# Inverse softmax divisors by broadcast loads from DRAM instead of products on TensorE

## The reference

```python
q, k, v = X @ Wq, X @ Wk, X @ Wv              # 16 heads of queries, 8 of keys and values, 64 wide
q, k = rope(q), rope(k)                       # each key head serves 2 query heads
att = 50 * tanh(q k^T / 16 / 50)              # causal
att = softmax(att)
x = layernorm(X + (att v) @ Wo)
q8 = per_token_int8(x)                        # scale = max|x| / 127
x = layernorm(x + float16((q8 @ weight^T) * in_scale * w_scale + bias))
```

## Time and profile before

| | us |
|---|---|
| median of 3 runs | 1320.56 (1318.67 to 1322.78) |
| the profiled execution | 1322.9, span 1321.2 |
| TensorE matmuls busy | 1272.4 (96% of the span), 5840 of them |
| weight loads busy | 936.2 (71%) |
| VectorE busy | 1038.7 (79%) |
| ScalarE busy | 901.4 (68%) |
| GpSimd busy | 377.7 (29%) |
| mean granted TensorE clock | 0.989 of 2.4 GHz |

### The profile page before, as it was taken

How to read it: one execution, slowest core, us unless ns; L and a number is a source line. 1 busy time by engine, 2 the same in 40 slices (tenths; PEclk the granted TensorE clock), 3 DMA queues, 4 the chain that set the end, 5 groups by cost and what they waited for, 6 DMA issues and landing times.

```text
span 1321.2 us, 17006 instructions
## 1 busy us (share of the span) xinstructions
PE 1272.4 (96%) x5840; PEld 936.2 (71%) x5840; DVE 1038.7 (79%) x1314; ACT 901.4 (68%) x1019; POOL 377.7 (29%) x438
## 2 busy tenths in 40 slices
PE   6899999999999999999999999999999999999896
PEld 5677777767766777677776777767777677777573
DVE  3588988983679888896478988898556988888566
ACT  4278787862677777875368867687447777879464
POOL 4232231111751111111383111111147211112165
PEclk9899999999999999999999999999999999999898
DMA  9683736495724464748551654466762355353551
GB/s 317 140 280 101 175 113 168 119 243 152 189 69 107 113 149 99 203 92 244 159 152 65 152 112 124 96 184 182 206 185 80 93 139 110 104 116 119 148 142 56
DMA packets 112401, 191.44 MB, mean 145 GB/s; under 512 B 19382, under 2 KB 65980, under 8 KB 104764
## 3 DMA queue, kind: packets, MB, share of 16 engines
q1 hardware_dynamic: 107564, 179.88, 52.1%
q10 hardware_dynamic: 4752, 10.49, 2.1%
HBM read 84.67 MB, written 38.54 MB: 93 GB/s over the span
## 4 chain that ended last, share of the span: by engine, by line
PE 83%; DVE 7%; issue 3%; ACT 3%; DMA 2%; POOL 1%; SPq 1%; POOLq 0%; DVEq 0%; ACTq 0%
PE ps L829 27%; PE ps L749 19%; PE ps L803 17%; PE ps L873 11%; PE ps L770 6%; PE ps L893 1%; PE ps L849 1%; DVE prob_lo L1292 1%; DVE prob_hi L1288 1%; DMA div<-y_scratch 1%; DVE xT L1208 1%; DVE stats L1370 1%; ACT probs L1032 1%; ACT probs L1027 0%; PE ps L883 0%
## 5 line engine op out<-in xcount | busy, mean ns | idle before, releaser
L829 PE MATMUL ps<-prob_hi,v 128*65 128x512 f32 (+3 forms) x1280 | 410.7, 371 | 8.4 <-DVE prob_lo L1292 8.4
L1027 ACT ACTIVATE probs<-ps 128x1024 f32<-128x1024 f32 x288 | 293.6, 1019 | 133.3 <-PE ps L803 133.3
L1292 DVE TENSOR_TENSOR prob_lo<-probs,prob_hi 128x1024 fp32r<-128x1024 f32 x288 | 360.0, 1250 | 9.8
L1535 POOL TENSOR_SCALAR_AFFINE_SELECT probs<-probs 128x256 f32<-128x256 f32 (+1 forms) x192 | 155.6, 818 | 705.3 <-ACT probs L1032 705.3
L803 PE MATMUL ps<-qk 128*128 128x512 f32 (+1 forms) x1280 | 314.5, 372 | 3.0 <-issue 1.8
L1032 ACT ACTIVATE probs<-probs 128x1024 f32<-128x1024 f32 x288 | 305.7, 1061 | 8.6
L749 PE MATMUL ps<-xT,w_ring 128*128 128x512 f32 x1152 | 286.9, 393 | 4.3 <-issue 4.3
L803 PEld LDWEIGHTS ps<-qk 128*128 128x128 f32 x1280 | 224.6, 189 | 62.6 <-issue 3.8
L1288 DVE CAST prob_hi<-probs 128x1024 fp32r<-128x1024 f32 x285 | 203.9, 715 | 79.7 <-POOL probs L1535 48.1
L749 PEld LDWEIGHTS ps<-xT,w_ring 128*128 128x128 f32 x1152 | 215.7, 189 | 50.9 <-issue 5.8
L829 PEld LDWEIGHTS ps<-prob_hi,v 128*65 128x65 f32 (+1 forms) x1280 | 170.7, 135 | 98.7 <-DVE prob_lo L1292 14.6
(11 more groups left out here) (92 smaller groups left out, 964.1 us busy)
## 6 DMA issues: line engine op xcount, KB each, us to landing
qk<-work_r SPq DMA_DIRECT2D x64, 512.0 KB, 8.8
qk<-work_r SPq DMA_DIRECT2D x256, 128.0 KB, 2.7
y_scratch<-sums SPq DMA_DIRECT2D x128, 130.0 KB
y_raw<-y_scratch SPq DMA_DIRECT2D x64, 256.0 KB, 4.3
wo<-wo_scratch SPq DMA_DIRECT2D x7, 2048.0 KB, 8.7
w_ring<-w_scratch SPq DMA_DIRECT2D x12, 1024.0 KB, 6.9
x_raw<-X_T SPq DMA_DIRECT2D x16, 512.0 KB, 6.7
x_in<-X SPq DMA_DIRECT2D x32, 256.0 KB, 4.3
```

What stands on the lines that cost most here:

```text
L829: mm = nc.tensor.matmul(sums_ps[:, :, GQ - w:GQ], v[:, kt, v0:v0 + width], p[:, at, col:col + REP * w].rearrange("p (h q) -> p h q", h=REP ...
L1027: nc.scalar.activation(probs[:, prob_place(g), :], scores[:, g % 2, :], ACT.Tanh, scale=SCORE_SCALE / SOFTCAP).then_inc(capped, 1)
L1292: nc.vector.tensor_tensor(prob_lo[:, prob_place(g), :], probs[:, prob_place(g), :], prob_hi[:, hi_place(g), :].bitcast(F32), ALU.subtract) ...
L1535: nc.gpsimd.affine_select(out=diag, in_=diag, compare_op=ALU.is_ge, fill=0.0, base=0, pattern=[[0, n], [1, P]], channel_multiplier=-1).the ...
```

## The change

`load_rows` now loads each head's row of inverse divisors, in fp32, to all 64 partitions of that head (a DRAM access pattern with step 0 over the partitions), so two DMAs of 256 KB per tile instead of two of 8 KB. There is one buffer `rows` of 128 x 8 x 128 fp32 for all tiles, so `load_rows(t)` waits for `scale_y(t - 1)`. `scale_y` multiplies `y_raw` by `rows` in SBUF. `invert` is the reciprocal alone, and `store_inverse` stores `div` in one DMA. `spread`, its set-up on GpSimd, VectorE and SP, and `spread_rows` are gone. On SP `load_rows(b, 1)` moves behind `put_sums` and `load_div` (in the last batch behind `put_sums(G - 2)`), and in the loop `load_rows(t + 3)` takes the place of `load_rows(t + 4)`. Two waits are renamed: `score(b, 1)` waits for `capped` of the batch before instead of its last `scale_y`, and the `rescale` of the last two tiles waits for the last `scale_y` instead of the last spread.

```diff
-    r_scratch = nc.dram_tensor("r_scratch", [2, G, KO * REP * GQ], F32, kind="Internal").ap()
+    r_scratch = nc.dram_tensor("r_scratch", [G, KO * REP * GQ], F32, kind="Internal").ap()
...
-        rows = over("rows", "work", [P, KO * P], F32R)
+        rows = over("rows", "work", [P, KO, P], F32)
...
             def store_inverse(b, c):
-                sp.wait_ge(inverse_lo, divs_upto(b, c))
-                for part in range(2):
-                    sp.dma_start(r_scratch[part, c].rearrange("(p n) -> p n", p=P),
-                                 inverse[:, part, :].bitcast(F32)).then_inc(div_stored[c], 16)
+                sp.wait_ge(inverse_done, divs_upto(b, c))
+                sp.dma_start(r_scratch[c].rearrange("(p n) -> p n", p=P), div[:, c, :]).then_inc(div_stored[c], 16)
...
             def load_rows(b, t):
-                sp.wait_ge(div_stored[t // 2], 32 * (b + 1))
-                if t >= 2:
-                    sp.wait_ge(rows_spread, rows_upto(b, t - 2))
-                for part in range(2):
-                    r0 = rows_at(t) + REP * part
-                    sp.dma_start(rows[r0:r0 + REP, :].rearrange("h (k n) -> h k n", k=KO).bitcast(F32),
-                                 r_scratch[part, t // 2].rearrange("(k h t n) -> t h k n", k=KO, h=REP, t=2)[t % 2]
-                                 ).then_inc(rows_loaded[t % 2], 16)
+                sp.wait_ge(div_stored[t // 2], 16 * (b + 1))
+                if t >= 1:
+                    sp.wait_ge(y_scaled, rows_upto(b, t - 1))
+                for h in range(REP):
+                    row = r_scratch[t // 2].rearrange("(k h t n) -> h t k n", k=KO, h=REP, t=2)[h, t % 2]
+                    sp.dma_start(rows[h * HD:(h + 1) * HD, :, :],
+                                 row.unsqueeze(0).broadcast_to([HD, KO, P])).then_inc(rows_loaded, 16)
...
                     load_rows(b, 0)
-                load_rows(b, 1)
                 store_inverse(b, 1)
...
                     load_div(b, 3)
+                    load_rows(b, 1)
                     load_y(b, 2)
                     for t in range(XRING):
                         load_x(b, t)
                     load_rows(b, 2)
-                    load_rows(b, 3)
                 else:
+                    load_rows(b, 1)
                     load_y(b, 2)
-                    load_rows(b, 2)
                     load_div(b, 2)
                     load_x(b, 0)
                     put_sums(b, NKV - 1, G - 1)
-                    load_rows(b, 3)
+                    load_rows(b, 2)
                     load_div(b, 3)
                     load_x(b, 1)
...
-                    if t + 4 < NT:
-                        load_rows(b, t + 4)
+                    if t + YRING < NT:
+                        load_rows(b, t + YRING)
...
-            def spread_rows(b, t):
...
-                for e in range(2):
-                    mm = nc.tensor.matmul(ps[:, spread_bank(b, t) + e, :], spread[rows_at(t):rows_at(t) + 2 * REP, :],
-                                          rows[rows_at(t):rows_at(t) + 2 * REP, e * 512:(e + 1) * 512], start=True, stop=True)
-                mm.then_inc(rows_spread, 1)
...
             def invert(b, c):
                 dve.wait_ge(div_loaded[c], 16 * (b + 1))
                 nc.vector.reciprocal(div[:, c, :], div[:, c, :]).then_inc(inverse_done, 1)
-                dve.wait_ge(inverse_done, divs_upto(b, c))
-                if divs_upto(b, c) > 1:
-                    before = divs_upto(b, c) - 2
-                    dve.wait_ge(div_stored[before % G], 32 * (before // G + 1))
-                nc.vector.tensor_copy(inverse[:, 0, :], div[:, c, :]).then_inc(inverse_hi, 1)
-                dve.wait_ge(inverse_hi, divs_upto(b, c))
-                nc.vector.tensor_tensor(inverse[:, 1, :], div[:, c, :], inverse[:, 0, :].bitcast(F32),
-                                        ALU.subtract).then_inc(inverse_lo, 1)
 
             def scale_y(b, t):
-                dve.wait_ge(rows_spread, rows_upto(b, t))
+                dve.wait_ge(rows_loaded, 32 * rows_upto(b, t))
                 dve.wait_ge(y_loaded[t % YRING], 2 * ring_upto(b, t, YRING))
                 row = y_raw[:, y_place(t), :, :].rearrange("p k n -> p (k n)")
-                nc.vector.tensor_tensor(row, ps[:, spread_bank(b, t):spread_bank(b, t) + 2, :].rearrange("p a c -> p (a c)"), row,
+                nc.vector.tensor_tensor(row, rows[:, :, :].rearrange("p k n -> p (k n)"), row,
                                         ALU.mult).then_inc(y_scaled, 1)
```

More of the change, by code:

```diff
@@ L168, in attention_block @@
         ident = over("ident", "div", [P, P], F32)
-        inverse = sb("inverse", [P, 2, P // G], F32R)
-        spread = sb("spread", [P, P], F32R)
-        spread_f32 = over("spread_f32", "prob_hi", [P, P], F32)
         ident16 = sb("ident16", [P, P], BF16)
@@ L191, in attention_block @@
         ps = ctx.enter_context(nc.psum_tensor("ps", [P, 8, 512], F32))
-        SPREAD_BANK, PV_BANK, PROJ_BANK = 2, 4, 6
+        PV_BANK, PROJ_BANK = 4, 6
         scores = ps[:, 0:4, :].rearrange("p (a h) c -> p a (h c)", a=2)
@@ L259, in attention_block @@
         inverse_done = sem("inverse_done")
[L260 to L266, removed]
+        rows_loaded = sem("rows_loaded")
         y_loaded = [sem(f"y_loaded{n}") for n in range(YRING)]
@@ L370, in v_bank @@
             return (PROJ_BANK + t % 2) if b == 0 or t < 2 or t >= NT - 2 else t % 2
[L373 to L378, removed]
         def row_tile(t):
@@ L591, in _ @@
             sp.dma_start(ffn_raw[:, :, :], ffn_weight_T.rearrange("(k p) c -> p k c", p=P)).then_inc(ffn_raw_in, 16)
-            sp.wait_ge(spread_set, 1)
-            for r0 in (REP, 32, 32 + REP):
-                sp.dma_start(spread[r0:r0 + REP, :].bitcast(F32), spread[0:REP, :].bitcast(F32)).then_inc(spread_ready, 16)
             sp.wait_ge(wv_hi_done, 2)
@@ L796, in score @@
                 elif g == 1:
-                    pe.wait_ge(y_scaled, rows_upto(b - 1, NT - 1))
+                    pe.wait_ge(capped, scores_upto(b - 1, NB - 1))
                 else:
@@ L928, in _ @@
                 weigh(b, NB - 2)
-                if not more:
-                    spread_rows(b, 0)
                 weigh(b, NB - 1)
@@ L936, in _ @@
                     project_v(b + 1, 3)
-                    spread_rows(b, 0)
                     project_v(b + 1, 4)
                     project_v(b + 1, 5)
-                spread_rows(b, 1)
                 if more:
@@ L945, in _ @@
                 for t in range(NT):
-                    if 1 <= t < NT - 1:
-                        spread_rows(b, t + 1)
                     for third in range(3):
@@ L1358, in rescale @@
                 if t >= NT - 2:
-                    dve.wait_ge(rows_spread, rows_upto(b, NT - 1))
+                    dve.wait_ge(y_scaled, rows_upto(b, NT - 1))
                 elif t >= FRING:
@@ L1389, in norm2 @@
                                         ).then_inc(normed, 1)
-            dve.wait_ge(spread_made, 2)
-            nc.vector.tensor_copy(spread[0:REP, :], spread_f32[0:REP, :]).then_inc(spread_set, 1)
             dve.wait_ge(const_made, 3)
@@ L1569, in _ @@
             nc.gpsimd.memset(one[:, :], 1.0).then_inc(const_made, 1)
-            nc.gpsimd.memset(spread_f32[0:REP, :], 1.0).then_inc(const_zero, 1)
-            pool.wait_ge(const_zero, 5)
+            pool.wait_ge(const_zero, 4)
             for i in (ident, ident16):
@@ L1574, in _ @@
                                         pattern=[[-1, P]], channel_multiplier=1).then_inc(const_made, 1)
-            nc.gpsimd.affine_select(out=spread_f32[0:REP, :], in_=spread_f32[0:REP, :], compare_op=ALU.is_ge, fill=0.0,
-                                    base=0, pattern=[[1, P]], channel_multiplier=-HD).then_inc(spread_made, 1)
-            pool.wait_ge(spread_made, 1)
-            nc.gpsimd.affine_select(out=spread_f32[0:REP, :], in_=spread_f32[0:REP, :], compare_op=ALU.is_ge, fill=0.0,
-                                    base=HD - 1, pattern=[[-1, P]], channel_multiplier=HD).then_inc(spread_made, 1)
             split_wk(0)
```

## The result

| | before | after |
|---|---|---|
| median of 3 runs, us | 1320.56 | 1369.48 (1365.73 to 1375.52) |
| ratio to before | | 1.0368, 95% interval 1.0326 to 1.0410 |
| profiled execution, us | 1322.9, span 1321.2 | 1365.7, span 1364.0 |
| TensorE busy | 1272.4 | 1258.1 |
| mean granted clock | 0.989 | 0.977 |

Slower by 3.7%. Lines of the kernel after: `load_rows` L492, `scale_y` L1260, `round_y` L1013, `round_v` L952, `split_v` L1165, `invert` L1254, `load_div` L478, `put_sums` L557, `project_out` L831, `turn_q` L841, `rescale` L1306, `residual2` L1501 and L1503, `w_scale` L689.

What follows compares the result with a forecast made beforehand. TensorE, busy 96% of the span, was taken to bound the kernel. Three batches at +9.3 us (+27.9) and the last at +0.6 gave +28.5 us, so 1320.6 + 28.5 = 1349 us; range 1325 to 1388.

Steps and rivals of the forecast that it cites:

- Products, 0.7 us a pair, 22 us at most: TensorE's 64 spread matmuls: each of 32 removed pairs gains 0.7 us where TensorE waits for nothing, 22 us at most.
- Start-up: 0: Kernel start: the removed set-up work on spread lies under the first loads, so it gains 0.
- Lock of the two SBUF inputs: Tile loop: scale_y with two SBUF inputs and GpSimd's add block each other; +0.4 us per batch for four tiles.
- tends to 7.65: Tiles with a residual2 and a scale_y: period no less than about 7.1 us, tending to 7.65, against 7.41.
- -0.6: Two tiles behind the weights' stretch in batches 0 to 2: pairs 6 and 7 against the lock, -0.6 us per batch.
- Row load 4.9 us from the first issue: Each tile's pair of row loads, priced like y_raw's loads: 4.9 us from the first issue to landing.
- Seam +3.1 in each batch: Batches 0 to 2: split_v(6) behind scale_y(1), which waits for rows(1), makes project_out(0) 3.1 us later.
- Clock, "a coin's toss, so +1.0": Seam: TensorE's idle 4.6 us may halve its clock, costing about 2 us; counted as +1.0 per batch.
- pair 2, -0.7: Batches 0 to 2, behind the seam's wait: removing pair 2 of the spread products gains 0.7 us.
- Weights +6.5 per batch with the clock: Batches 0 to 2: rows(4) and rows(5) collide with 2 MB of weights, +5.6 us, plus +0.9 for another idle stretch.
- Last batch +0.6: Last batch, without seam or weights: +2.1 for bytes, -0.5 shorter inversion, -1.4 pairs 2 and 3, +0.4 lock.
- slow reading of one place: Rival, chance 0.25: reading one DRAM place is slow; 1374 us at 150 GB/s, about 1415 at 104 GB/s.

Runs made afterwards that it cites:

- e1: Changed kernel without row loads, y multiplied by two PSUM banks (result not divided by the sums): 0.9824 of the kernel before, 1299.1 us.
- e2: Changed kernel without row loads, y multiplied by the cosine table in SBUF (result not divided by the sums): 0.9936 of the kernel before, 1312.7 us.
- e3: Changed kernel with all row loads and waits, but y multiplied by two PSUM banks instead of the rows: 1.0334 of the kernel before, 1365.6 us.
- e6: Changed kernel with all four weight loads asked for ahead of load_rows(4): 1.0378 of the kernel before, 1372.3 us.
- e9: Changed kernel, split_v/round_v(6, 7) ahead of scale_y(1)/round_y(1), w_scale and bias ahead of load_rows(4), wk and wq at t = 4: 1.0092, 1333.1 us.
- e8: Changed kernel, row loads reading 64 different rows of y_scratch, y multiplied by the cosine table: 1.0323 of the kernel before, 1364.7 us.
- e7: Changed kernel, each row load cut to one of eight pieces (64 KB per tile), y multiplied by the cosine table: 1.0150, 1343.5 us.
- e10: Changed kernel with rows(1), (4) and (5) of batches 0 to 2 issued by ScalarE on its own queue: 1.0285 of the kernel before, 1357.7 us.
- e11: Changed kernel, rows(1) ahead of div(2), e9's weight order; last batch div(1) ahead of rows(0), second buffer for odd rows: 1.0043, 1327.1 us.

## Why the prediction was right and wrong

Right in sign and in the main in mechanism (order, meeting, clock); 1349 us was 20 us too low, and 1369.5 lies within 1325 to 1388. Point by point:

- *Products, 0.7 us a pair, 22 us at most*: right of the tile, 0.8 us where nothing else holds it up. e1's 23 us are in part luck: 9 of them lie at the start and ahead of the last tile loop.
- *Start-up: 0*: this was 2 us too little a gain. The first of the 288 `prob_lo` starts at 61.3 instead of 63.1, the last of batch 0 2.0 us sooner; of the change, only the set-up of `spread` lies there, though no run takes it out alone:

```profile
L1244 DVE TENSOR_TENSOR prob_lo<-probs,prob_hi x288: 1218/1226/2202, 61.3 to 1276.4; 128x1024 fp32r<-128x1024 f32 x144
```

- *Lock of the two SBUF inputs*: "tends to 7.65" was measured at 7.67 and 7.68 us, and e2 and e3 show it on and off. The sum took it at +0.4 us per batch for four tiles; from turn_q(3) to turn_q(6) the loop lost 0.5 to 0.9 us where the sum had -0.6 for the part of it. That is 3.7 us too little over three batches. 1.3 of them are the size: I counted 7.51 per tile, between the ends of 7.1 and 7.65, and it was the upper end. The other 2.4 are a slip in the sum: by 7.51 against 7.41 two such tiles cost +0.2 us, and -0.6 stands there.
- *Row load 4.9 us from the first issue*: 5.55 in batch 0's seam (315.37 to 320.92); it was issued 0.56 us sooner than forecast, so `project_out(0)` started at 324.59, with 324.7 forecast. TensorE idled 6.7 us instead of 4.6 because it was done 2.2 us sooner than I had it, nearly all of it the start-up's 2.0.
- *Seam +3.1 in each batch*: this step failed, and batch 0's +3.0 is luck. From the last `prob_lo` of a batch to `project_out(0)` the seam is 5.0, 4.6 and 6.2 us longer than before; in batch 0 the start-up's 2.0 us hide that, in batches 1 and 2 the scores add 0.6 each. I set the new order against batch 0's times of before and left out that the 512 KB of rows(0) now stand ahead of `wo` and `put_sums`, on which div(2) waits. Batch 1, SP's queue, before and after:

```profile
625.17 0.41 SPq L577 DMA_DIRECT2D y_scratch<-sums  x1
...
632.80 0.32 SPq L495 DMA_DIRECT2D div<-y_scratch  x1
```

```profile
638.29 0.40 SPq L557 DMA_DIRECT2D y_scratch<-sums  x1
...
647.58 0.32 SPq L478 DMA_DIRECT2D div<-y_scratch  x1
```

  7.6 us have become 9.3 (7.4 and 8.4 in batch 0, 7.6 and 9.7 in batch 2), and rows(1) is behind that. Against the loops before, 14.9 us in place of 9.3: 5.6 us too little.
- *Clock, "a coin's toss, so +1.0"*, and *pair 2, -0.7*: the clock fell in every one of the three seams and cost 2.35, 2.3 and 1.5 us. Pair 2 gave nothing there: from `project_out(0)` to turn_q(0) the kernel before and e1 both take 12.34 us. Together 5.3 us too little, 3.2 of the clock and 2.1 of the pair. The half price had no row behind it; the trace of before had one idle stretch of that length and a fall behind it.
- *Weights +6.5 per batch with the clock*: 7.1, 3.6 and 6.7 us; 2.1 us too much in all. The size was right, the path only in part: I had only y(5) and rows(5) in it, and left out that `rescale(0)` waits for `w_scale` ahead of `scale_y(4)` (4.9, 3.2, 3.2 us). e6 and e9 show that this is a wait of its own.
- *Last batch +0.6*: 2.4 us; 1.8 too little. Up to `project_out(0)` it is +1.4 (div(1) took 11.5 us to its use instead of 10.1), about the forecast's 2.1 - 0.5. The step left out is the one behind it, +1.3 up to turn_q(0): div(3) stands behind rows(1) and rows(2) on SP's queue, rows(2) waits for `scale_y(1)` (issued at 1293.57), and div(3) was asked for 7.7 us after the start of `project_out(0)` instead of 5.6. VectorE waits for it, where it didn't before, ahead of the shift that q of tile 0 needs, and TensorE waits for q:

```profile
1299.68 0.35 DVE L1254 RECIPROCAL div<-div 128x32 f32<-128x32 f32 x1 [2.36 <-DMA div<-y_scratch]
...
1303.84 0.40 PE L841 MATMUL ps<-ident,q 128*128 128x128 bf16 x4 [2.87 <-ACT q L1029]
```

These differences (3.7, 5.6, 5.3, -2.1 and 1.8; the start-up is inside the seam's) make up the 14.3 us between the forecast's 28.5 and the spans' 42.8. The other 6 us between 1349 and 1369.5 lie between the medians and the profiled executions: 3.8 below the median after, 2.3 above it before.

Of the rivals, *slow reading of one place* had the nearest number, 1374, for a reason that e8 doesn't bear out: a load from 64 places lands only 0.5 us sooner, and from tile 3 on of the last batch rows were used 5.3 to 6.1 us after their issue, between the forecast's 4.9 and the rival's 6.3. *Seam and lock alone* fails on the weights (17.4 us). What e7, e9 and e10 leave open is how the 14 us between e11 (1327.1) and e2 (1312.7) divide among the bytes, the other loads that they delay, and the clock.

## What to carry to other kernels

When a transfer grows from a few KB to half a MB, redo the order of its queue, for every load behind it: here three quarters of the loss (36 of 49 us) came back by moving issues and two pieces of work, with no byte less, though no order made up for the bytes. A wait that moves to the front of an in-order engine is priced by what stands behind it on that engine, not by its own length. And measure a stage from its own start, in every batch: absolute times of the first one hid 2 of the seam's 5 us behind a gain made elsewhere.

## What the runs showed of the hardware that was not expected

- A queue of its own gave a load no way past 2 MB that another queue had asked for 3 us before: 13.4 and 16.2 us to its use in e10, against 4.5 us from issue to landing at the median of that run's row loads on SP's queue.
- A load of an eighth of the bytes takes more than half the time at the median (2.5 against 4.6 us to its landing), and still 10.8 us to its use behind the 2 MB.
- Where GpSimd and VectorE meet, the one that starts 0.04 us later waits for the other in full: 2.33 us for an add of 1.30.
